# Cross-attention's value sums of half a batch: one piece of twelve key blocks in place of three pieces of four

## The reference

```python
def step(t, p):                       # six times
    tn = _ln(t, norm_g, norm_b)
    t = _mha(tn, tn, skv, sq, sow, sob, tgt_mask) + t      # self-attention, 16 heads of 64
    tn = _ln(t, norm_g, norm_b)
    t = _mha(src, tn, ckv, cq, cow, cob, src_mask) + t     # cross-attention on the 375 context tokens
    tn = _ln(t, pg, pb)
    t = t + (jax.nn.relu(tn @ w1 + b1) @ w2 + b2)
```

## Time and profile before

| | |
|---|---|
| median of three runs | 3152.71 us |
| profiled execution, its own time | 3159.5 us |
| its span, first to last instruction | 3157.7 us |
| mean granted clock of TensorE | 0.963 of full speed |
| PE / DVE / ACT / POOL busy | 92% / 53% / 41% / 30% |
| one body, from its first score tile to the next body's | 116.3 to 119.1 us, once 122.0 |

### The profile page before, as it was taken

The page is one execution under the profiler, slowest core; times in us unless marked ns, Lnnn a source line. Parts: engine busy times, 40 slices in busy tenths (PEclk is TensorE's granted clock), DMA queues, the critical chain, the costliest instruction groups (busy, mean ns, idle before and its releaser), DMA issues.

```text
span 3157.7 us, 72157 instructions
## 1 busy us (share of the span) xinstructions
PE 2910.2 (92%) x23656; PEld 2337.1 (74%) x23656; DVE 1678.7 (53%) x6361; ACT 1300.5 (41%) x4274; POOL 963.0 (30%) x1169
## 2 busy tenths in 40 slices
PE   6675899999999999999999999999999999999999
PEld 4454778778778768778778778778778778777777
DVE  2342546546546546546546546546546546545555
ACT  2222335335335335335335335335344434444444
POOL 0000324324324324324324323323323323323323
PEclk9887899999999999999999999999999999999999
DMA  4002011031111021111022111022111022111010
GB/s 151 26 0 81 1 27 27 2 83 42 55 27 27 2 83 47 50 27 27 2 83 58 39 27 27 2 83 65 32 27 27 2 83 66 31 27 27 2 27 13
DMA packets 132313, 121.56 MB, mean 38 GB/s; under 512 B 15261, under 2 KB 121318, under 8 KB 130278
## 3 DMA queue, kind: packets, MB, share of 16 engines
q1 hardware_dynamic: 131942, 116.53, 14.4%
HBM read 115.59 MB, written 0.92 MB: 37 GB/s over the span
## 4 chain that ended last, share of the span: by engine, by line
issue 51%; POOL 24%; PE 20%; DVE 2%; ACT 1%; POOLq 1%; DMA 0%; SPq 0%; DVEq 0%; ACTq 0%
POOL prob L541 17%; PE proj L581 8%; PE proj L601 3%; POOL prob L511 3%; PE sum L601 3%; PE sum L769 2%; POOL ctx_parts L532 1%; PE proj L573 1%; POOL tw L491 1%; PE score L745 1%; PE tr L756 1%; PE sum L581 1%; DVE qcT L1191 1%; POOLq L540 1%; POOL ctx_parts L529 1%
## 5 line engine op out<-in xcount | busy, mean ns | idle before, releaser
L541 POOL TENSOR_TENSOR prob<-prob,rtotal 128x375 f32<-128x375 f32 x672 | 543.4, 812 | 750.0 <-DVE rtotal L1451 749.0
L961 ACT ACTIVATE prob<-prob,negmax 128x375 f32<-128x375 f32 (+1 forms) x688 | 418.8, 609 | 452.3 <-DVE negmax L1442 421.6
L884 PE MATMUL sum<-pT,ctx 32*128 32x224 f32 (+1 forms) x4608 | 500.6, 358 | 12.6 <-DVE qcT L1434 12.6
L884 PE MATMUL tr<-pT,ctx 32*128 32x224 f32 (+1 forms) x4608 | 500.6, 358 | 0.0
L884 PEld LDWEIGHTS sum<-pT,ctx 32*128 32x128 f32 (+1 forms) x4608 | 417.7, 185 | 73.2 <-issue 53.7
L1442 DVE CUSTOM_DVE_ANT_0 prob<-score,cbias 128x375 f32<-128x375 f32 x672 | 358.3, 533 | 193.5 <-PE score L581 192.1
L884 PEld LDWEIGHTS tr<-pT,ctx 32*128 32x128 f32 (+1 forms) x4608 | 417.0, 185 | 0.0
L581 PE MATMUL score<-ctx_parts,qc_high 128*128 128x376 f32 x1344 | 412.5, 388 | 0.0
L1460 DVE STREAM_TRANSPOSE pT<-prob 128x384 f32<-128x384 f32 x672 | 373.9, 560 | 0.0
L511 POOL TENSOR_TENSOR prob<-prob,rtotal 112x448 f32<-112x448 f32 x200 | 186.4, 932 | 575.8 <-DVE rtotal L1318 575.8
L1032 ACT ACTIVATE prob<-prob,negmax 112x112 f32<-112x112 f32 x800 | 298.9, 377 | 86.3 <-DVE negmax L1336 86.2
(11 more groups left out here) (170 smaller groups left out, 5009.6 us busy)
## 6 DMA issues: line engine op xcount, KB each, us to landing
ctx<-ctx SPq DMA_DIRECT2D x192, 176.0 KB
w_kv<-sa_kv SPq DMA_DIRECT2D x6, 2048.0 KB, 10.0
f<-ff_w SPq DMA_DIRECT2D x12, 1024.0 KB, 9.5
cmask<-ctx_mask SPq DMA_DIRECT2D x24, 375.0 KB, 4.5
w_q<-sa_q SPq DMA_DIRECT2D x6, 1024.0 KB, 11.0
w_o<-sa_ow SPq DMA_DIRECT2D x6, 1024.0 KB, 6.5
c_q<-ca_q SPq DMA_DIRECT2D x6, 1024.0 KB, 7.8
c_o<-ca_ow SPq DMA_DIRECT2D x6, 1024.0 KB, 10.4
```

Source lines behind the costliest of these rows:

```text
L541: pool.tensor_tensor(row, row, rtotal[:, G * SG + i:G * SG + i + 1].broadcast_to([P, S2]), ALU.mult).then_inc(prob_ready, 1)
L884: ins = pe.matmul(bank[:, 0:HT * R], ctx4[keys_of, m // (HALVES // NB), j, :], pT[keys_of, m % 2, :, j * R:(j + 1) * R], start=j == 0, sto ...
L961: act.activation(o, i, ACT.Exp, bias=negmax[0:rows, col:col + 1], scale=scale, accum_out=total[0:rows, col:col + 1]).then_inc(exp_ready, 1)
```

## The change

The three pieces of a half become one piece of twelve key blocks. It stands in step 7m+13, where the second of the three stood. The last half, already without a break, is one piece in step 32. The copies of finished sums of halves 0 and 1 move two steps ahead, to steps 14 and 21.

```diff
-    PIECES = 3
+    PIECES = 1
...
-    SUM_STEPS = {HT * m + t: (m, i) for m in range(HALVES - 1) for i, t in enumerate((11, 13, 15))}
+    SUM_STEPS = {HT * m + t: (m, i) for m in range(HALVES - 1) for i, t in enumerate((13,))}
     SUM_STEPS.update({NT + 4 + i: (HALVES - 1, i) for i in range(PIECES)})
-    TAKE_STEPS = {HT * m + 16: m for m in range(HALVES - 2)}
+    TAKE_STEPS = {HT * m + 14: m for m in range(HALVES - 2)}
```

## The result

The changed kernel takes 3164.31 us (median of 20 runs, 3143.53 to 3184.40), against 3150.92 us before (20 runs, 3147.19 to 3157.02). The ratio is 1.0041, with a 95% interval of 1.0025 to 1.0056: slower by 13 us (8 to 18). The forecast was 17 us slower, within 3150 to 3190.

A forecast was written before the change was run, and what follows sets the result against it. TensorE, 92% busy, was taken to set the pace. Per body 3.61 us lost against 2.81 saved, 0.71 by direct sum; 24 bodies make 17 us, so the median goes from 3152.7 to about 3170, range 3150 to 3190.

The forecast's parts named there:

- Borders and the wait for the copies: Five borders at 0.40, 0.21 in step 29 and TensorE's 0.60 wait in step 25 go: 2.81 us saved per body.
- TensorE runs two tiles ahead of VectorE at most: Score tiles without pieces between: two banks make each wait for the maximum two tiles back; 3.61 us lost per body.
- The price of a wait: A waiting score tile starts 0.60 us after the maximum two tiles back starts; bounds +6 to +29 us in all.
- L: Start of a score tile's third matmul on TensorE; 0.34 us after its first in an unbroken stream, 0.45 after a wait.
- S: Start of a score tile's first matmul on TensorE; the later of TensorE's own time and maximum t-2 plus 0.60 us.
- First and second stretch: Score tiles before the first piece, then tiles 14 to 20 before the second: waits lose 1.02 and 0.67 us per body.
- Third stretch: From tile 21 to tile 27, before the third piece: tiles 24 to 27 all wait, losing 1.92 us per body.
- No transposition is held back either: Halves 0 and 1 are summed two steps before `pT` is needed again, so no delay to transpositions was counted.
- The clock, 7 us to either side: Half speed after each loop turn lasts 3.4 or 6.8 us, 12 times each; four cases more or fewer are 7 us.
- (a): Rival: borders win, faster; 3085 us if TensorE never waited for VectorE, 3128 with half the waits gone; chance 0.08.
- (b): Rival: no measurable change; waits at their least price with a favourable mix of clock phases, 3150 to 3162 us; chance 0.22.
- (c): Rival: clock falls to half speed around tiles 24 to 27, 1.7 us per body, 41 in all, about 3211; chance 0.04.

The follow-up runs named there:

- four-piece kernel: Kernel before with four pieces of three key blocks, in steps 7m+11, +12, +13 and +15, instead of three pieces; one run 3180.81 us beside 3157.99.
- the earlier copies: Kernel before with the copies of sums one step earlier, in steps 15 and 22; one run 3133.5 us beside 3158.0.

## Why the prediction was right, and where it was not

- **Borders and the wait for the copies, 2.81 us saved.** Right. The four-piece kernel gives 0.41 per border (0.40 predicted), the earlier copies give 0.58 (0.60 predicted).
- **TensorE runs two tiles ahead of VectorE at most, so bare tiles wait.** Right, and shown: with no instruction of PE changed, a faster VectorE took 1.64 us off the stage. The price of a wait, a start 0.60 behind the maximum's and L 0.45 behind S, rested on one case and held: tile 13 starts at 13.79 and has its L 0.45 later. The profile lists five of the eight waits reckoned with, those of tiles 13, 19, 25, 26 and 27; the shorter ones hide behind the recorded end of the matmul before. Tiles 12, 17 and 24 start 12.50, 22.43 and 34.63 behind the first, where 12.51, 22.48 and 34.72 were forecast.
- **First and second stretch, 1.02 and 0.67 us lost.** Right, within 0.04 us at tile 21.
- **Third stretch, 1.92 us lost.** Mis-sized. The step of tile 24 was taken as one with plain work, 1.00 as before, and it measured 1.42. "No transposition is held back either" holds for the sums themselves; but in that step the four waits for them take 0.4 us of VectorE's time although they have long been fulfilled, which they did not while the copies of sums stood in step 23. So the stage grew by 1.03 us, not 0.71.
- **The clock, 7 us to either side.** Mis-sized. The mix before was read nearly right: 12 short and 11 long falls at the 23 turns, where 12 of each were named. But the clock gave about 12 us back (24.7 less 13), and in the profiled execution about 31 (half of 62.5 us). The prediction counted only a change between long and short falls and didn't reckon with turns that have none. The two errors had opposite signs, and that 17 stands so near 13 is luck: with the clock as it was before, the result would have been about 25.
- **The rivals.** (a), borders win, is out for one piece and true for two. (b), no change, is not quite out: 13 us is over the 9.5 named as what can be told from no change, but the interval begins at 8. Of its two conditions the clock's favourable mix came about and the least price of a wait didn't. (c), the clock falls in the thin stretch, happened in one body of 24. Windows of the twelfth body, first tiles 25 and 26 up to the fall, then from tile 25 to the value projections:

```profile
1685.00:1688.60 3.60, 2.25 (x11) 1.32 (x10) 3.31 (x14) 2.01 (x7) 2.34 (x4) 1.00 0.01 2
...
1686.00:1700.00 14.00, 12.87 (x165) 10.76 (x167) 8.79 (x41) 5.50 (x21) 4.57 (x6) 0.88 0.01 2
```

PE was busy for 2.25 of the 3.60 us ahead of the fall. That body's stage was 53.04 us, 1.6 over the median, where the rival wanted 1.7 in every body. The Trainium skill (TensorE: Matmul & The Clock Gate, A second HAM failure mode) tells of such falls from short idle times between groups of matmuls; the trace agrees in this one body only. A fall away from the turn is nothing new in itself: the kernel before has one too, 112.8 us behind the first score tile of its seventh body, after a single wait of PE of 2.25 us.

## What to carry to other kernels

In this kernel a long unbroken piece of matmuls saves changes of shape but starves the engine that follows; afterwards TensorE goes at that engine's pace for as long as it has no other work to put between. Lay both engines out step by step from their own rows: the piece should be no longer than the follower's backlog lasts, here half of what was tried. And when instructions move away, ask what they were hiding, fulfilled waits included.

Where the clock depends on pauses, judge a schedule by the stage's length in the trace first, and only then by the total: here the clock took back half of the 24.7 us that the change added.

## What had not been expected of the hardware

- Four fulfilled waits, each with an addition to a semaphore, pass 0.11 us apart on VectorE. They cost it 0.40 us in one step (24), 0.05 in another of the same kernel (17), and nothing in the kernel before.
- Pauses of 3.0 to 3.8 us at the loop's turn are followed by half speed at 23 of 23 turns before and, at the same lengths, at 13 of 23 after. 1.15 us of work added to each body cost 0.7 (0.5 to 0.95).
- Equal executions of one program lie within 10 us with one length of the body and within 41 with another, and the granted clock of a run goes with its time: 0.979 at 3143.5 us, 0.965 at 3184.4. Which lengths are favourable, and why, these runs leave open.
